# Two queue positions exchanged in an attention tower: the product with the values and the scores on TensorE, the heads' evictions and the relu on ScalarE

## Chip, core and metric

The kernel runs on one core of one Trainium2 chip. The metric is the device time of one execution in microseconds (us).

## What is computed

64 images of 196 tokens (patches of 16x16x3 pixels) go through patch embedding and layer norm, one quantised attention layer with a residual, and a layer of routed experts with a residual. What matters here is the attention, cut from the reference:

```
q = fake_quant(q, s_q, -4, 3) * scale          # 12 heads of 16 columns
k = fake_quant(k, s_k, -4, 3)
v = fake_quant(v, s_v, -4, 3)
attn = einsum('bhnd,bhmd->bhnm', q, k)         # the scores
attn = fake_quant(attn / N, s_attn, 0, 7)      # clipped at 0 and 7, rounded; no softmax
out = einsum('bhnm,bhmd->bhnd', attn, v)       # the product with the values
out = fake_quant(out, s_after, -4, 3)
return out @ Wproj.T + bproj
```

## The kernel before

The images are taken in 16 groups of four (784 tokens). A group passes through three stages in three consecutive passes, so that in each pass one group is embedded and normalised (`one`), the next older one goes through attention (`two`), and the oldest through projection and experts (`three`). There are 18 passes. A pass has 24 slots, and written-out tables say in which slot each piece of work is issued. Every engine runs through the slots in its own program order, and semaphores tie the engines together. An engine never passes over an instruction that waits.

A unit of attention is two heads of one image; a group has 24 units, so slot s of a pass holds unit s. The work of a unit:

- TensorE, `qk`, in even slots: 8 small matmuls make the scores of two units, s and s+1. They fill all four banks of `scores_ps`, so `qk` waits until ScalarE has read the two units before (`act_relu`).
- ScalarE, `relu`, in every slot: the scores of unit s times a scale, clipped at 0, rounded into `relu16`. It waits for `qk` and for VectorE's reading of the unit before last.
- VectorE, `quantise`, one slot later: clips at 7 and writes `prob`, a ring of 8 units.

When the six units of an image are in `prob`, their product with the values follows. The table `AV = [8, 14, 20, 26]` gives its slots for the four images; 26 is slot 2 of the next pass. All four slots are even, so each of them holds a `qk` as well, as long as a group is in stage two:

- TensorE, `av`: 24 small matmuls write the heads of one image into `near_ps`. It waits for `prob`, for the values, and for `near_ps` to be empty. That bank is shared with the patch embedding (`embed`), whose tiles ScalarE moves out as the last thing of a slot (`embed_evac`, L861).
- ScalarE, `heads_evac`: two activations, `o16_a` (L920) and `o16_b` (L921), move the heads out.
- VectorE, `clip_heads`, at the end of the slot, clips them for the projection.

In the slot before three of the four `av` (slots 1, 7 and 13) an embedded tile ends on TensorE and is moved out by ScalarE. In slot 20 `near_ps` has long been empty.

The rest of TensorE's program order in a slot, behind `qk` and `av`: the first layer of the experts (`up`, L777), transposes (`turn`, L663), query, key and value rows (`step`, L641), embedding (L650, its last matmul L655), the routing (L751 to L753), `down` (L787), `project` (L741). Behind `relu` and `heads_evac`, ScalarE has `gelu` (L932), the copies of the transposed rows (L876, L886), `norm1` (L867), `step_evac` (L908, L913) and `embed_evac`. VectorE has among others the split of transposed rows (L1151), which waits for ScalarE's copies.

Of the kernel before, what the change touches and what calls it, by code (L numbers as in the profile page):

```python
# [117 lines left out]
def stages(i):  # L118

    return [Group(i - back) if 0 <= i - back < GROUPS else None for back in range(3)]  # L120


def wait(eng, sem, value):

    if value > 0:
        eng.wait_ge(sem, value)
# [106 lines left out]
def at(slots, slot):  # L233
    return [t for t, s in enumerate(slots) if s == slot]
# [7 lines left out]
def second_at(table, two, three, slot):  # L242

    return [(g, g.first2 + t) for g, s in ((two, slot), (three, slot + SLOTS)) if g for t in at(table[g.n2], s)]
# [7 lines left out]
def heads_at(two, three, slot):  # L252
    return [(g, n) for g, s in ((two, slot), (three, slot + SLOTS)) if g for n in at(AV, s)]
# [41 lines left out]
def vit_tower_kernel(nc, x, tok_w, tok_b, ln_w, ln_b, w_qkv, w_proj, s_q, s_k, s_v, s_attn,  # L295
# [5 lines left out]
    with ctx:  # L301
# [179 lines left out]
        for i in range(GROUPS + 2):  # L481
            one, two, three = stages(i)
# [13 lines left out]
        for i in range(GROUPS + 2):  # L496
            one, two, three = stages(i)
# [36 lines left out]
        def empty(eng, *user):  # L534

            if user in USER_BEFORE:
                eng.wait_ge(*USER_BEFORE[user])
# [40 lines left out]
        def is_first(g):  # L578
            return g.offset == 0
# [40 lines left out]
        def _(pe):  # L620
            ident = const_sb[0:TT, C_IDENT:C_IDENT + TT]

            def router_product():

                come(pe, 3)
                pe.wait_ge(rows_out, EVACS)
                pe.matmul(product_ps[:, 0:EXPERTS], encw[:, 0:128], sww[:, :], start=True, stop=True)
                pe.matmul(product_ps[:, EXPERTS:2 * EXPERTS], encw[:, 128:EMBED + LO], sww[:, :],
                          start=True, stop=True)
                pe.matmul(product_ps[0:TT, 2 * EXPERTS:3 * EXPERTS], encb[:, 0:1].broadcast_to([HIDDEN, TT]),  # L630
                          sww[:, :], start=True, stop=True).then_inc(set_pe, 1)
# [25 lines left out]
            def turn(kind, tile):  # L657
                src, made = (xn2, dve_xn2) if kind == 1 else (xn3, dve_xn3)

                pe.wait_ge(made, tile + 1)  # L660
                wait(pe, dve_lo, TURN_NO[kind, tile])
                rows = src[:, tile % 2]
                pe.transpose(turn_ps[:, 0:TT], rows[:, 0:128], ident)  # L663
                pe.transpose(turn_ps[0:LO, TT:2 * TT], rows[:, 128:EMBED], ident).then_inc(turned, 1)  # L664
# [47 lines left out]
            def unit_of(pair, odd):  # L712

                return 2 * odd + pair // 2 if pair < 4 else 4 + odd

            def av(g, n):

                pe.wait_ge(prob_out, g.count(SLOTS, PAIRS * (n + 1)))
                pe.wait_ge(v_clip, g.count(GI, n + 1))
                empty(pe, "heads", g.offset, n)  # L720
                def product(row, col, pair, odd, c, start, stop):
                    u = PAIRS * n + unit_of(pair, odd)
                    return pe.matmul(near_ps[row:row + 32, col:col + SEQ], v_pad[:, 2 * n + c, pair, odd],  # L723
                                     prob[:, u % RING, pair % 2, c * SEQ:(c + 1) * SEQ], start=start, stop=stop)

                for odd, c in itertools.product(range(2), repeat=2):
                    for pair in range(4):
                        product(32 * pair, 0, pair, odd, c, odd + c == 0, odd + c == 2)
                for c in range(2):
                    for pair, odd in itertools.product(range(4, PAIRS), range(2)):  # L730
                        last = product(64 * (pair - 4) + 32 * odd, SEQ, pair, odd, c, c == 0, c == 1)
                last.then_inc(av_made, 1)
# [59 lines left out]
            def body(one, two, three):  # L792
                for s in range(SLOTS):

                    if one and is_first(one) and s == min(FIRST_STEPS):
                        pe.wait_ge(set_dve, SET_ATTENTION)
                    if two and is_first(two) and s == ROUTER_PRODUCT:
                        router_product()
                    if two and is_first(two) and s == PROJ[two.n2][0]:
                        pe.wait_ge(set_dve, SET_ALL)  # L800
                    if two and s % VISIT == 0:
                        qk(two, s // VISIT)
                    for g, n in heads_at(two, three, s):
                        av(g, n)
                    if three and s <= LAST_EMBED:
                        for n in at(UP, s):
                            up(three, n)
                    for g, tile in second_at(TURN3, two, three, s):
                        turn(2, tile)
                    for tile in first_at(TURN2, one, s):  # L810
                        turn(1, tile)
                    if one and s in FIRST_STEPS:
                        step(one, FIRST_STEPS[s])
                    work = embeds_of(one, s) if one else []
                    ahead = 0 if any((k - s) % SLOTS == 0 for k in AV) else 1
                    for tile, j in work[:ahead]:
                        embed(tile, j)
                    if three and s > LAST_EMBED:
                        for n in at(UP, s):
                            up(three, n)  # L820
                    if three:
                        for part in at(ROUTE, s):
                            route(three, part)
                    if two and s in SECOND_STEPS:
                        step(two, SECOND_STEPS[s])
                    if s > LAST_EMBED:
                        for tile in third_at(DOWN, three, s):
                            down(three, tile)
                    if three:
                        for part in at(SPREAD, s):  # L830
                            spread_choice(three, part)
                    for g, tile in second_at(PROJ, two, three, s):
                        project(g, tile)
                    for tile, j in work[ahead:]:
                        embed(tile, j)
                    if s <= LAST_EMBED:
                        for tile in third_at(DOWN, three, s):
                            down(three, tile)
# [13 lines left out]
        def _(act):  # L852
# [63 lines left out]
            def heads_evac(g, n):  # L916
                cols = slice(SEQ * n, SEQ * (n + 1))
                act.wait_ge(av_made, g.count(GI, n + 1))
                wait(act, heads_clip, g.count(GI, n + 1 - GI))
                act.activation(o16_a[:, cols], near_ps[:, 0:SEQ], ACT.Identity, scale=c_out[:, :])  # L920
                act.activation(o16_b[:, cols], near_ps[:, SEQ:2 * SEQ], ACT.Identity,  # L921
                               scale=c_out[:, :], bias=one_row[:, :]).then_inc(heads_out, 1)
# [11 lines left out]

            def body(one, two, three):
                for s in range(SLOTS):
                    if two:
                        relu(two, s)
                    for g, n in heads_at(two, three, s):
                        heads_evac(g, n)  # L940
                    if three and s <= LAST_EMBED:
                        for n in at(UP, s):
                            gelu(three, n)
                    if two and is_first(two) and s == PROJ[two.n2][0]:
                        come(act, 3)
                    for g, tile in second_at(TURN3, two, three, s):
                        high_experts(g, tile)
                    for tile in first_at(TURN2, one, s):
                        high_rows(tile)
                    for tile in first_at(NORM1, one, s):  # L950
                        norm1(tile)
                    if one and is_first(one) and s == min(FIRST_STEPS):
                        act.wait_ge(set_dve, SET_ATTENTION)
                    if one and s in FIRST_STEPS:
                        step_evac(one, FIRST_STEPS[s])
                    if three and s > LAST_EMBED:
                        for n in at(UP, s):
                            gelu(three, n)
                    if two and s in SECOND_STEPS:
                        step_evac(two, SECOND_STEPS[s])  # L960
                    for tile in first_at(EVAC1, one, s):
                        embed_evac(tile)
# [425 lines left out]
```

## Time and profile before

| | |
|---|---|
| median of 3 runs | 998.43 us (997.61 to 999.94) |
| the profiled execution | 998.46 us, of which the span is 996.7 us |
| TensorE matmul busy | 907.5 us, 91% of the span |
| VectorE busy | 743.0 us, 75% |
| ScalarE busy | 702.9 us, 71% |
| GpSimd busy | 510.8 us, 51% |
| mean granted clock of TensorE | 0.972 of full speed |

Busy time is summed over instructions. Matmuls overlap in the pipeline, so the busy share of TensorE is not its share of peak. "Idle" is the time an engine stood still ahead of an instruction, with the instruction that released it; "issue" is idle time with no releaser in sight.

### The profile page before, as it was taken

Reading aid. Unit: us, or ns where it says so; the run is one execution under the profiler, and the core shown is the slowest. Engines: PE = TensorE matmul, PEld = TensorE weight load, DVE = VectorE, ACT = ScalarE, POOL = GpSimd, SP = SyncE. Lnnn points to the kernel's source line nnn. Section 1 sums busy time; section 2 is a strip of 40 time slices with the busy share of each in tenths; the row PEclk is TensorE's granted clock in tenths of the full one; section 3 lists DMA queues with packets and bytes.
Section 4 is the critical chain, followed back from the end, with each engine's and each line's share of the span. In section 5 each row is a group of like instructions: output and inputs, shape, how many; then the busy total and the mean of one; then the engine's idle time right before and its main releaser. Section 6 shows DMA issues by size and latency. Waiting matters only on the chain.

```text
span 996.7 us, 24830 instructions
## 1 busy us (share of the span) xinstructions
PE 907.5 (91%) x8170; PEld 785.2 (79%) x8170; DVE 743.0 (75%) x2855; ACT 702.9 (71%) x1516; POOL 510.8 (51%) x890
## 2 busy tenths in 40 slices
PE   5678999999999999998889899999999999999877
PEld 4566888888888888877677788888888888887766
DVE  4677878788788778777676777878878877878563
ACT  1367877777878777776566777777787877777652
POOL 4434564637465564636527456463746556463332
PEclk9797999999999999999999999999999999999889
DMA  7321121212121121212102112121202111000000
GB/s 228 105 64 34 49 64 41 61 45 74 32 69 49 53 65 41 61 45 68 44 25 73 32 53 65 41 64 42 77 29 69 50 53 49 10 13 13 14 13 28
DMA packets 31395, 52.52 MB, mean 53 GB/s; under 512 B 4653, under 2 KB 17949, under 8 KB 31269
## 3 DMA queue, kind: packets, MB, share of 16 engines
q1 hardware_dynamic: 31268, 50.94, 16.7%
q8 instruction: 67, 1.10, 0.5%
q14 instruction: 60, 0.48, 0.2%
HBM read 41.30 MB, written 9.63 MB: 51 GB/s over the span
## 4 chain that ended last, share of the span: by engine, by line
PE 34%; DVE 6%; ACT 6%; issue 5%; POOL 1%; DVEq 0%; ACTq 0%; POOLq 0%
PE mixed_ps L787 7%; PE near_ps L650 6%; PE mixed_ps L777 6%; PE mixed_ps L641 5%; PE scores_ps L708 2%; ACT relu L897 2%; PE near_ps L723 1%; PE turn_ps L663 1%; ACT hid L932 1%; ACT o_b L921 1%; DVE h L1222 1%; PE turn_ps L664 1%; PE mixed_ps L741 1%; DVE k_b L1182 1%; PE mixed_ps L742 1%
## 5 line engine op out<-in xcount | busy, mean ns | idle before, releaser
L897 ACT ACTIVATE relu<-scores_ps,c_prob 98x784 uint16<-98x784 f32 x384 | 348.8, 909 | 139.2 <-PE scores_ps L708 117.3
L650 PE MATMUL near_ps<-we,x_sb 128*128 128x192 f32 x1176 | 258.4, 341 | 12.5 <-DMA const_sb<-in_const 8.2
L978 POOL TENSOR_TENSOR ve<-mv,const_sb 128x1 f32<-128x1 f32 x294 | 60.3, 205 | 360.9 <-DVE mv L1319 357.1
L650 PEld LDWEIGHTS near_ps<-we,x_sb 128*128 128x128 f32 x1176 | 195.2, 196 | 19.1 <-DMA const_sb<-in_const 8.2
L991 POOL TENSOR_TENSOR expd<-econst,below 128x8 f32<-128x8 f32 x98 | 161.9, 1666 | 49.6 <-DVE below L1249 49.6
L981 POOL TENSOR_TENSOR rs<-ve,const_sb 128x1 f32<-128x1 f32 x294 | 173.9, 591 | 23.0
L1160 DVE TENSOR_SCALAR prob<-relu 98x784 bf16<-98x784 uint16 x384 | 151.1, 394 | 9.4 <-ACT relu L897 1.2
L787 PE MATMUL mixed_ps<-w_sb,hid 128*128 128x192 f32 x784 | 145.8, 330 | 0.0
L787 PEld LDWEIGHTS mixed_ps<-w_sb,hid 128*128 128x128 f32 x784 | 125.5, 191 | 1.4
L1135 DVE TENSOR_SCALAR xn<-h,mv,rs 128x192 f32<-128x192 f32 x196 | 74.1, 378 | 33.9 <-POOL rs L981 33.7
L932 ACT ACTIVATE hid<-mixed_ps,b_sb 128x384 f32<-128x384 f32 (+1 forms) x128 | 73.0, 586 | 36.2 <-PE mixed_ps L777 35.7
L1121 DVE BATCH_NORM_STATS2 st<-h 128x6 f32<-128x192 f32 x196 | 70.1, 357 | 10.8 <-POOL h L1000 6.9
L663 PE MATMUL turn_ps<-const_sb,xn 128*128 128x128 f32 x196 | 60.2, 307 | 17.6 <-DVE xn L1135 7.8
L996 POOL TENSOR_TENSOR m<-n,lnw 128x192 f32<-128x192 f32 x98 | 59.0, 602 | 33.1 <-ACT n L867 32.5
L908 ACT ACTIVATE rows<-mixed_ps,inv_rows 128x392 int16<-128x392 f32 x96 | 55.9, 582 | 24.6 <-PE mixed_ps L641 24.1
L867 ACT ACTIVATE n<-y,nb,rs 128x192 f32<-128x192 f32 x98 | 52.8, 539 | 23.1 <-DVE nb L1116 23.0
L1289 DVE SCALAR_TENSOR_TENSOR out_sb<-mixed_ps,pmax,h 128x192 f32<-128x192 f32 x98 | 40.9, 418 | 35.3 <-PE mixed_ps L787 32.5
L1000 POOL TENSOR_TENSOR h<-m,lnb 128x192 f32<-128x192 f32 x98 | 58.7, 599 | 7.7
L861 ACT ACTIVATE y<-near_ps 128x192 f32<-128x192 f32 x98 | 32.0, 326 | 42.0 <-PE near_ps L655 38.9
L708 PE MATMUL scores_ps<-q_a,k_a 32*98 32x196 bf16 x1024 | 49.0, 266 | 12.7 <-ACT relu L897 12.3
L741 PE MATMUL mixed_ps<-wp_a,o_a 128*128 128x192 f32 x196 | 55.7, 309 | 3.5 <-DVE o_b L1209 1.2
L663 PEld LDWEIGHTS turn_ps<-const_sb,xn 128*128 128x128 f32 x196 | 27.9, 143 | 39.0 <-DVE xn L1135 20.4
(155 smaller groups left out, 2208.2 us busy)
## 6 DMA issues: line engine op xcount, KB each, us to landing
x_sb<-in_x SPq DMA_DIRECT2D x98, 384.0 KB, 3.0
out<-out_sb SPq DMA_DIRECT2D x98, 96.0 KB, 1.6
we<-in_tok_w SPq DMA_DIRECT2D x1, 576.0 KB, 4.3
w_sb<-in_w SPq DMA_DIRECT2D x1, 384.0 KB
hid<-in_w_qkv SPq DMA_DIRECT2D x1, 288.0 KB, 5.5
hid<-in_w_qkv SPq DMA_DIRECT2D x2, 144.0 KB, 5.7
hid<-in_w SPq DMA_DIRECT2D x1, 256.0 KB
hid<-in_w SPq DMA_DIRECT2D x2, 128.0 KB
```

The costliest lines, as they stand in the source:

```text
L650: pe.matmul(dst, x_sb[:, tile % X_RING, j], we[:, j], start=j == 0, stop=False)
L663: pe.transpose(turn_ps[:, 0:TT], rows[:, 0:128], ident)
L708: last = pe.matmul(scores_ps[0:KEYS, bank, c * SEQ:(c + 1) * SEQ], keys, q[rows, n * SEQ:(n + 1) * SEQ], start=True, stop=True)
L741: pe.matmul(dst, o_a[:, cols], wp_a[:, j], start=j == 0, stop=False)
L787: last = pe.matmul(dst, hid[:, m, cols], w2_sb[:, m], start=False, stop=m == FC - 1)
L897: act.activation(relu16[:, u % 2], scores_ps[0:KEYS, 2 * (u % VISIT):2 * (u % VISIT) + 2, 0:2 * SEQ], ACT.Relu, scale=c_prob[0:KEYS, :]).t ...
L932: act.activation(hid[:, m, cols], bank[:, 0:cols.stop - cols.start], ACT.Gelu, bias=b1_sb[:, m:m + 1]).then_inc(gelu_out, 1)
L981: pool.tensor_tensor(rs[:, t], ve[:, t], const_sb[0:TT, C_HALFNEG:C_HALFNEG + 1], ALU.pow).then_inc(rs_sem, 1)
L991: pool.tensor_tensor(expd[:, t], econst[:, t], below[:, t], ALU.pow).then_inc(pool_exp, 1)
L1121: dve.bn_stats(st[:, tile % NT], src[:, tile % H_RING]).then_inc(st_sem, 1)
L1135: dve.tensor_scalar(dst[:, tile % 2], src[:, tile % H_RING], mv[:, t, 0:1], rs[:, t], ALU.subtract, ALU.mult).then_inc(dst_sem, 1)
L1160: dve.tensor_scalar(prob[:, u % RING], relu16[:, u % 2], 7.0, None, ALU.min).then_inc(prob_out, 1)
```

## The change

In a slot that has both, `av` is issued ahead of `qk` on TensorE, and `heads_evac` ahead of `relu` on ScalarE. No instruction is added or removed, and no table is changed.

```diff
@@ TensorE, body @@
+                    for g, n in heads_at(two, three, s):
+                        av(g, n)
                     if two and s % VISIT == 0:
                         qk(two, s // VISIT)
-                    for g, n in heads_at(two, three, s):
-                        av(g, n)
@@ ScalarE, body @@
                 for s in range(SLOTS):
+                    for g, n in heads_at(two, three, s):
+                        heads_evac(g, n)
                     if two:
                         relu(two, s)
-                    for g, n in heads_at(two, three, s):
-                        heads_evac(g, n)
```

## Rows read from the trace of the kernel before

**Rows 1.** The page's first part: busy us, share of the span, instructions.

```profile
PE 907.5 (91%) x8170; PEld 785.2 (79%) x8170; DVE 743.0 (75%) x2855; ACT 702.9 (71%) x1516; POOL 510.8 (51%) x890
```

**Rows 2.** Stages: stretch, length, busy time by engine, PEclk (granted clock), DMA.

```profile
121.00:177.00 56.00, 53.89 (x514) 47.29 (x510) 44.65 (x175) 43.45 (x95) 30.87 (x55) 1.00 0.18 54
461.00:532.00 71.00, 59.58 (x513) 50.63 (x505) 47.56 (x180) 45.17 (x99) 33.34 (x59) 0.95 0.14 43
```

**Rows 3.** Groups by line: busy us, mean ns | idle before, releasers.

```profile
L897 ACT ACTIVATE relu<-scores_ps,c_prob 98x784 uint16<-98x784 f32 x384 | 348.8, 909 | 139.2 <-PE scores_ps L708 117.3 <-DVE prob L1160 19.3
...
L723 PE MATMUL near_ps<-prob,v_pad 98*32 98x196 bf16 x1536 | 45.2, 252 | 8.0 <-ACT y L861 6.3 <-DVE v_pad L1193 0.2 <-DVE prob L1160 0.2
```

**Rows 4.** Timeline, slots 1 to 3: start us, duration us, engine, line, [idle before].

```profile
217.86 0.25 PE L655 MATMUL near_ps<-rows,first 128*128 128x192 bf16 x1
...
218.04 0.38 PE L708 MATMUL scores_ps<-q_a,k_a 32*98 32x196 bf16 x8
...
218.15 0.33 ACT L861 ACTIVATE y<-near_ps 128x192 f32<-128x192 f32 x1
...
218.62 0.70 PE L723 MATMUL near_ps<-prob,v_pad 98*32 98x196 bf16 x24 [0.21 <-ACT y L861]
...
219.25 0.28 PE L751 MATMUL mixed_ps<-wr_a,f_hi 128*128 128x16 f32 x1
...
219.37 0.42 ACT L920 ACTIVATE o_a<-near_ps,c_out 128x196 int16<-128x196 f32 x1
...
220.09 0.92 ACT L897 ACTIVATE relu<-scores_ps,c_prob 98x784 uint16<-98x784 f32 x1
...
220.77 0.35 DVE L1160 TENSOR_SCALAR prob<-relu 98x784 bf16<-98x784 uint16 x1
...
221.84 0.59 ACT L908 ACTIVATE rows<-mixed_ps,inv_rows 128x392 int16<-128x392 f32 x1 [0.84 <-PE mixed_ps L641]
```

**Rows 5.** Timeline, slots 20 to 22 of the same pass.

```profile
205.14 0.38 PE L708 MATMUL scores_ps<-q_a,k_a 32*98 32x196 bf16 x8
...
205.44 0.70 PE L723 MATMUL near_ps<-prob,v_pad 98*32 98x196 bf16 x24
...
205.57 0.91 ACT L897 ACTIVATE relu<-scores_ps,c_prob 98x784 uint16<-98x784 f32 x1 [1.19 <-PE scores_ps L708]
...
206.08 0.33 PE L663 MATMUL turn_ps<-const_sb,xn 128*128 128x128 f32 x1
...
206.38 0.42 ACT L920 ACTIVATE o_a<-near_ps,c_out 128x196 int16<-128x196 f32 x1
...
207.09 0.28 ACT L886 ACTIVATE f_hi<-turn_ps 128x128 fp32r<-128x128 f32 x1
...
208.80 0.37 PE L708 MATMUL scores_ps<-q_b,k_b 32*98 32x196 bf16 x8 [0.96 <-ACT relu L897]
```

**Rows 6.** Timeline, slots 8 to 10 of the pass before.

```profile
178.66 0.58 ACT L932 ACTIVATE hid<-mixed_ps,b_sb 128x384 f32<-128x384 f32 x1 [0.23 <-PE mixed_ps L777]
...
179.81 0.89 ACT L897 ACTIVATE relu<-scores_ps,c_prob 98x784 uint16<-98x784 f32 x1
...
180.95 0.38 PE L708 MATMUL scores_ps<-q_b,k_b 32*98 32x196 bf16 x8
```

**Rows 7.** Timeline, slots 14 and 15.

```profile
191.05 0.70 PE L723 MATMUL near_ps<-prob,v_pad 98*32 98x196 bf16 x24
...
192.87 0.58 ACT L932 ACTIVATE hid<-mixed_ps,b_sb 128x384 f32<-128x384 f32 x1 [0.25 <-PE mixed_ps L777]
...
193.56 0.39 PE L777 MATMUL mixed_ps<-f_hi,w_hi_a 128*128 128x384 f32 x1
```

**Rows 8.** Timeline, TensorE's waits in the first and the last pass with attention.

```profile
67.78 2.58 PE L650 MATMUL near_ps<-we,x_sb 128*128 128x192 f32 x7 [1.21 <-ACT o_b L921]
...
941.40 0.37 PE L708 MATMUL scores_ps<-q_a,k_a 32*98 32x196 bf16 x8 [0.83 <-ACT relu L897]
...
955.14 0.36 PE L741 MATMUL mixed_ps<-wp_a,o_a 128*128 128x192 f32 x1 [1.21 <-DVE o_b L1209]
```

## The prediction

> **What bounds the kernel.** I read the page's first part, then the stages, then the groups by line, and last the timeline round each place where both pieces of work meet. The first part says that TensorE is busy for 91% of the span, far ahead of the others [rows 1]. The stages say that this is steady: apart from the start, the end and some 130 us in the middle, a pass takes 56 us, with TensorE busy for 53.9 of them at the full granted clock of 1.00 [rows 2]. So TensorE's own order is the clock of the kernel. A delay put into it stays, unless TensorE waits soon after for something that was not delayed too. The groups by line say where the two edited places stand. ScalarE stood idle 139 us ahead of its relus, 117 us of them for the scores, so it mostly runs behind TensorE and not ahead of it. `av` waited 6.3 us in all, for ScalarE's move of the embedded tile [rows 3].
>
> **The change, place by place.** No instruction comes or goes and SyncE's queue is untouched; the two exchanges are all. They happen 63 times: 16 in slot 8, 16 in 14, 16 in 20, and 15 in slot 2 (the last group's fourth product has no scores beside it). The durations, from the rows: from the start of `qk` to the start of what follows it, 205.14 to 205.44 = 0.30 us; from the start of `av` to the next, 205.44 to 206.08 = 0.64; `heads_evac` holds ScalarE from 219.37 to 220.09 = 0.72; a relu from 205.57 to 206.38 = 0.81 [rows 4, 5].
>
> *Slot 2.* The embedding's last matmul starts at 217.86. `qk` starts at 218.04 and runs while ScalarE moves the embedded tile out (218.15 to 218.48). `av` can't start before that bank is free: it starts at 218.62 and TensorE goes on at 219.25 [rows 4]. So before, `qk` lies in the shadow of a wait that has to be sat out anyway. With `av` first nothing covers that wait. `av` still starts at 218.62, `qk` follows at 219.25, and the rest goes on at 219.55: +0.30 us on TensorE. ScalarE: the heads start at 219.37 as before, since `av` ends as before, but ScalarE stands idle until then and the relu is still to come. Relu 2 ends at 220.09 + 0.91 = 221.00 and relu 3 starts at 220.90. ScalarE's next work, the rows at 221.84, waited 0.84 us for TensorE, and this hides relu 3 up to 221.71. Without that cover the path would get 0.81, not 0.30. On VectorE, `quantise` at 220.77 would have to wait until 221.04, +0.27 [rows 4]. Both stay within TensorE's +0.30.
>
> *Slot 8.* The same picture, +0.30. ScalarE has less cover: gelu waited 0.23 us [rows 6], so it moves by 0.81 - 0.23 = 0.58 at most, and some 0.5 where TensorE's product comes 0.3 later anyway. Relu 9 then ends at about 180.70 + 0.5 = 181.2, and the next `qk` would start at 181.25 without it. I take +0.31.
>
> *Slot 14.* `av` starts at 191.05 either way and `qk` costs +0.30. But gelu moves from 192.87 to about 193.32, ends near 193.90, and TensorE's third `up` in the row, at 193.56, writes the bank which that gelu empties. It starts near 193.96 in place of 193.86: +0.40 in all [rows 7].
>
> *Slot 20.* `near_ps` is empty here, so the exchange is free on TensorE itself. ScalarE is the path: it is idle until `qk` ends, does relu 20 at 205.57, the heads at 206.38, goes on at 207.09, and the `qk` of slot 22 has waited 0.96 us for relu 21 at the end of that row [rows 5]. Now ScalarE waits for `av`. `av` is done 0.70 after its start, at 205.84, the heads start at 205.89, which is 0.32 behind the 205.57 of before; heads and relu take as long in either order, so relu 21 and the `qk` of slot 22 come 0.32 later. TensorE waits 1.28 instead of 0.96: +0.32.
>
> The sum for a pass is 0.30 + 0.31 + 0.40 + 0.32 = 1.33 us. Of the 63 places 56 lie in the 14 passes between the start and the end: 14 x 1.33 = 18.6 us. The bounds for one place: nothing, if the delay is taken up by slack behind it, and 0.72 to 0.81, if the relu's whole delay reaches TensorE. I stay near 0.3 because all the waits between these places that I followed are themselves started by TensorE, so they move with it.
>
> **The tile shapes.** One transition isn't in this trace: `av` (98 rows by 32 columns of the array) straight into `qk` (32 by 98) and from there into full matmuls. Eight score matmuls as such take about 0.13 us: the group lasts 0.38, and one matmul of 196 columns 0.25, which is the mean of L723 [rows 3, 5]. The other 0.17 of the 0.30 passes before the next starts. If that 0.17 overlapped behind `av`, three places would cost 0.13 each, and a pass 0.8. I take 0.30, since `qk` straight into `av`, the same switch the other way round, shows the full 0.30 at 205.14 [rows 5]. The Trainium skill, page "TensorEngine Tiling (Array Packing)", section "Key Properties", says that changing the tiling mode drains the engine. By that rule every one of the three switches keeps its 0.17 and the pass costs 1.33 us; without it the cost is 0.8, or 11 us for the 14 passes. The trace agrees as far as it goes, by the 0.17 behind both kinds.
>
> **Start and end.** Here the heads come sooner and something waits for them. The embedding at 67.78 waited 1.21 us for the heads' move. At 955.14 the projection waited 1.21 us for heads that start 0.75 and not 1.24 us after the slot's begin: 0.5 us gained at each. At 941.40 `qk` waited 0.83 us for a relu, time that `av` now fills, worth some 0.4 us [rows 8]. The other four places I put at +0.5 together. That makes -0.9 us for start and end.
>
> The sum is 18.6 - 0.9 = 17.7 us. On the profiled execution, 998.46 us (1.8 of them outside the span and untouched), that makes 1016.2; the median of the runs is 998.43, the same within 0.03. I predict **1016 us**.
>
> **Rivals.**
>
> *Faster: `av` fills the waits for the relu.* `qk` waits for ScalarE to empty `scores_ps`, and `av` could run meanwhile and hand over the heads sooner. It decides if, at these four places, the relu is what TensorE waits for. At slot 20, `qk` doesn't wait, and at slots 2, 8 and 14 `av` waits for ScalarE longer than `qk` does. If slack behind took up all the delay and only the gains of start and end were left, it would be 998.4 - 1.4 = 997; with 0.3 us gained in slots 14 and 20 of each of the 14 passes as well (8.4), 989. Against it speaks that TensorE is busy 53.9 of 56 us [rows 2].
>
> *No change.* TensorE's delay is taken up, since the 0.96 us wait in slot 22 is there in every pass. That would need relu 21 not to move; but the row shows that the chain behind it begins with TensorE's scores. 998.
>
> *Half.* The switch from `av` to `qk` overlaps, or one of the four places is absorbed: 0.8 us a pass, 14 x 0.8 - 0.9 = 10.3, so 1009.
>
> *More.* The relu's delay reaches TensorE in slots 8 and 14, through `qk` in slot 10 or through VectorE, which splits transposed rows only after ScalarE's copies: 0.5 us for each place, 56 x 0.5 = 28, less 0.9: 1026.
>
> *The clock.* In the slow stretch in the middle the granted clock is 0.95, after long waits of TensorE, while it is 1.00 in passes whose longest wait is 0.96 [rows 2, 5]. If 1.28 us were enough to make it fall in each pass, the stretch at half clock would cost more than 1 us a pass, so over 1030.
>
> **How the numbers follow.** The forecast, between 1.1 and 1.6 us a pass (1013 to 1020), has 0.50; half 0.17; more 0.14; the clock 0.04; no change 0.06; faster 0.07; the rest, 0.02, is slower by only a few us. The range leaves out the cases without a delay and those of the clock: it reaches from 0.5 us a pass less the ends' gain (1004) to that of the whole 0.5 us a place (1026). I can tell 0.2%, or 2 us, from no change. Faster 0.07, same 0.06, slower 0.87.
>
> **What would show it.** In the profile after: L723 idle ahead of it grows from 8 us by some 0.3 us in each of three places of a pass, to 20 us or more, nearly all released by L861; the `qk` of the same slot follows 0.63 us behind `av` without a wait; the matmul behind comes 0.30 us after `qk`; TensorE's wait for relu in slot 22 is 1.28 us; heads start 0.75 us after the slot's first small matmul in slot 20; the steady pass takes 57.3 us and not 56.0. The prediction is wrong if steady passes still take 56.0 us, if `qk` behind `av` takes under 0.2 us, or if TensorE gets new waits for L932, L897 or VectorE's splits of 0.3 us or more.

## The result, and the profile after

The changed kernel takes 1020.99 us in the median of 4 runs (1019.71 to 1023.24), beside 998.02 us for the kernel before in the runs taken with it. The ratio is 1.0235, with a 95% interval of 1.0208 to 1.0262: slower. The forecast was 1016 us in a range of 1004 to 1026. One run in this document, the slowest with TensorE's exchange alone, was in a slower state and is left out of its ratio.

The page of the changed kernel, first part:

```profile
span 1021.5 us, 24830 instructions
...
PE 911.7 (89%) x8170; PEld 787.5 (77%) x8170; DVE 743.4 (73%) x2855; ACT 697.7 (68%) x1516; POOL 511.9 (50%) x890
```

The work is the same; each engine is busy about as long as before [rows 1], and the span is 24.8 us longer. So most of the difference is idle time. By stages, a steady pass and the slow stretch in the middle (stretch, length, busy time by engine, granted clock, DMA):

```profile
181.00:238.50 57.50, 54.05 (x508) 47.23 (x507) 44.65 (x175) 43.05 (x95) 31.00 (x55) 1.00 0.18 53
```

```profile
459.00:536.00 77.00, 64.14 (x548) 54.74 (x547) 52.83 (x200) 46.16 (x105) 35.96 (x64) 0.94 0.15 45
```

The steady pass grew from 56.0 to 57.5 us with the same TensorE work (53.9 and 54.1 us), still at the full clock [rows 2].

The groups by line show where TensorE and ScalarE now stand idle:

```profile
L920 ACT ACTIVATE o_a<-near_ps,c_out 128x196 int16<-128x196 f32 x64 | 27.1, 424 | 64.1 <-PE near_ps L723 64.1
...
L723 PE MATMUL near_ps<-prob,v_pad 98*32 98x196 bf16 x1536 | 44.7, 250 | 23.2 <-ACT y L861 22.3
```

TensorE's idle time ahead of `av` rose from 8.0 to 23.2 us, 22.3 of them for the embedded tile [rows 3]; ScalarE's ahead of the heads rose from 0.6 to 64.1 us.

Slot 2 after, TensorE, ScalarE and VectorE (start us, duration, [idle before]):

```profile
224.29 0.25 PE L655 MATMUL near_ps<-rows,first 128*128 128x192 bf16 x1
...
224.57 0.33 ACT L861 ACTIVATE y<-near_ps 128x192 f32<-128x192 f32 x1
...
225.04 0.70 PE L723 MATMUL near_ps<-prob,v_pad 98*32 98x196 bf16 x24 [0.51 <-ACT y L861]
...
225.67 0.38 PE L708 MATMUL scores_ps<-q_a,k_a 32*98 32x196 bf16 x8
...
225.79 0.42 ACT L920 ACTIVATE o_a<-near_ps,c_out 128x196 int16<-128x196 f32 x1 [0.89 <-PE near_ps L723]
...
225.98 0.28 PE L751 MATMUL mixed_ps<-wr_a,f_hi 128*128 128x16 f32 x1
...
227.53 0.36 DVE L1160 TENSOR_SCALAR prob<-relu 98x784 bf16<-98x784 uint16 x1 [0.25 <-ACT relu L897]
...
228.09 0.18 DVE L1243 TENSOR_TENSOR logit<-mixed_ps,logit 128x24 f32<-128x24 f32 x1
...
228.42 0.33 PE L741 MATMUL mixed_ps<-wp_a,o_a 128*128 128x192 f32 x1
```

From the embedding's last matmul to `av` it is 0.75 us, as before (0.76 in [rows 4]). The scores that used to run inside this wait now come 0.63 us behind `av`, and the routing starts 0.31 us behind them: 1.69 us from L655 to L751, 1.39 before. That is +0.30 us on TensorE at this place. At the same time VectorE waited 0.25 us for the relu, a wait that it did not have. Which of the two delays reaches the rest of the pass, these rows alone don't say.

Slots 20 and 22 after:

```profile
211.25 0.70 PE L723 MATMUL near_ps<-prob,v_pad 98*32 98x196 bf16 x24
...
211.89 0.38 PE L708 MATMUL scores_ps<-q_a,k_a 32*98 32x196 bf16 x8
...
212.01 0.42 ACT L920 ACTIVATE o_a<-near_ps,c_out 128x196 int16<-128x196 f32 x1 [1.49 <-PE near_ps L723]
...
212.73 0.91 ACT L897 ACTIVATE relu<-scores_ps,c_prob 98x784 uint16<-98x784 f32 x1
...
215.24 0.38 PE L708 MATMUL scores_ps<-q_b,k_b 32*98 32x196 bf16 x8 [1.28 <-ACT relu L897]
```

The heads start 0.76 us after the slot's first matmul, and TensorE's wait in slot 22 is 1.28 us, where [rows 5] has 0.96.

Slot 14 after (PEld is the weight load of the third product):

```profile
196.71 0.70 PE L723 MATMUL near_ps<-prob,v_pad 98*32 98x196 bf16 x24 [0.51 <-ACT y L861]
...
198.98 0.59 ACT L932 ACTIVATE hid<-mixed_ps,b_sb 128x384 f32<-128x384 f32 x1
...
199.62 0.19 PEld L777 LDWEIGHTS mixed_ps<-f_hi,w_hi_a 128*128 128x128 f32 x1 [0.28 <-ACT hid L932]
```

Gelu ends at 198.98 + 0.59 = 199.57, and the third product, which overwrites its bank, starts at 199.62 (its matmul and its weight load alike). That is 2.91 us behind `av`, and 2.51 before [rows 7].

To place the loss I took the starts of all `qk` from both traces and compared each interval from one to the next, averaged over five steady passes (passes 4 to 8 of the 18). The growth per place, in us, with that of each experiment below; the intervals around a place are summed, and a row's places can miss its sum by some 0.01. The two rows of one exchange alone are not at full clock throughout; what that does to them is said below.

| kernel | slot 2 | slot 8 | slot 14 | slot 20 and 22 | a pass |
|---|---|---|---|---|---|
| after | +0.33 | +0.34 | +0.46 | +0.32 | +1.46 |
| ScalarE's exchange alone | +0.33 | +0.35 | +0.45 | +0.90 | +2.03 |
| TensorE's exchange alone | +2.29 | +0.99 | +0.77 | +0.63 | +4.68 |
| both, slot 2 only | +0.33 | 0 | 0 | 0 | +0.34 |
| both, slot 14 only | 0 | 0 | +0.45 | 0 | +0.45 |
| both, slot 20 only | 0 | 0 | 0 | +0.32 | +0.32 |
| both, short relu, against its pair | +0.16 | +0.21 | +0.29 | -0.17 | +0.49 |
| heads of slot 20 out in slot 21 | 0 | 0 | 0 | +0.69 | +0.68 |

### The profile page after: what moved, and what is told of

It reads as the page before. It is cut to its first block, busy times and chain, and to the rows that moved or that the text cites. A ratio compares the mean times of both kernels' runs of the same rounds, so it can differ in the third digit from the quotient of the medians.

```text
span 1021.5 us, 24830 instructions
## 1 busy us (share of the span) xinstructions
PE 911.7 (89%) x8170; PEld 787.5 (77%) x8170; DVE 743.4 (73%) x2855; ACT 697.7 (68%) x1516; POOL 511.9 (50%) x890
## 4 chain that ended last, share of the span: by engine, by line
PE 34%; ACT 7%; DVE 6%; issue 5%; POOL 1%; DVEq 0%; ACTq 0%; POOLq 0%
PE mixed_ps L787 7%; PE near_ps L650 6%; PE mixed_ps L777 6%; PE mixed_ps L641 5%; ACT relu L897 3%; PE near_ps L723 2%; PE scores_ps L708 2%; PE turn_ps L663 1%; ACT hid L932 1%; DVE k_b L1182 1%; PE turn_ps L664 1%; DVE prob L1160 1%; DVE h L1222 1%; ACT y L861 1%; PE mixed_ps L741 1%
## 5 line engine op out<-in xcount | busy, mean ns | idle before, releaser
L650 PE MATMUL near_ps<-we,x_sb 128*128 128x192 f32 x1176 | 261.9, 345 | 12.1 <-DMA const_sb<-in_const 8.4
L978 POOL TENSOR_TENSOR ve<-mv,const_sb 128x1 f32<-128x1 f32 x294 | 63.8, 217 | 379.6 <-DVE mv L1319 376.0
L650 PEld LDWEIGHTS near_ps<-we,x_sb 128*128 128x128 f32 x1176 | 198.0, 198 | 18.9 <-DMA const_sb<-in_const 8.4
L981 POOL TENSOR_TENSOR rs<-ve,const_sb 128x1 f32<-128x1 f32 x294 | 171.6, 584 | 23.0
L1160 DVE TENSOR_SCALAR prob<-relu 98x784 bf16<-98x784 uint16 x384 | 151.2, 394 | 19.5 <-ACT relu L897 11.3
L996 POOL TENSOR_TENSOR m<-n,lnw 128x192 f32<-128x192 f32 x98 | 59.1, 603 | 33.3 <-ACT n L867 32.7
L920 ACT ACTIVATE o_a<-near_ps,c_out 128x196 int16<-128x196 f32 x64 | 27.1, 424 | 64.1 <-PE near_ps L723 64.1
L723 PE MATMUL near_ps<-prob,v_pad 98*32 98x196 bf16 x1536 | 44.7, 250 | 23.2 <-ACT y L861 22.3
L723 PEld LDWEIGHTS near_ps<-prob,v_pad 98*32 98x32 bf16 x1536 | 31.0, 96 | 39.7 <-issue 28.2
```

Source lines behind the costliest of these rows:

```text
L650: pe.matmul(dst, x_sb[:, tile % X_RING, j], we[:, j], start=j == 0, stop=False)
L978: pool.tensor_tensor(ve[:, t], mv[:, t, 1:2], const_sb[0:TT, C_EPS:C_EPS + 1], ALU.add).then_inc(ve_sem, 1)
L981: pool.tensor_tensor(rs[:, t], ve[:, t], const_sb[0:TT, C_HALFNEG:C_HALFNEG + 1], ALU.pow).then_inc(rs_sem, 1)
L1160: dve.tensor_scalar(prob[:, u % RING], relu16[:, u % 2], 7.0, None, ALU.min).then_inc(prob_out, 1)
```

## The experiments

**The halves of the change.** TensorE's exchange alone:

```diff
 # TensorE
+ for g, n in heads_at(two, three, s): av(g, n)
  if two and s % VISIT == 0: qk(two, s // VISIT)
- for g, n in heads_at(two, three, s): av(g, n)
 # ScalarE: unchanged, relu ahead of heads_evac
```

> Only TensorE's order is exchanged; ScalarE still does the relu ahead of the heads. My theory (TensorE pays in slots 2, 8 and 14 because nothing covers the wait for the embedded tile any more, and in slot 20 because ScalarE starts later): slot 2 +0.3 us, slot 8 +0.5, slot 14 +0.7, slot 20 +0.63 (the relu now starts behind the scores, which are 0.63 later), 2.1 us a pass, +30 us in all, some 1028. The rival (the exchange on ScalarE costs, since it pushes the relu back; the exchange on TensorE is free): a change of less than 5 us.

Measured: 1073.71 us (1061.78 to 1078.8, 4 runs), ratio 1.0727 (1.0665 to 1.079). Far from free, so the rival falls, but it is also more than twice what I expected. Slot 2 alone shows 2.29 us in the table:

```profile
226.73 0.70 PE L723 MATMUL near_ps<-prob,v_pad 98*32 98x196 bf16 x24 [0.51 <-ACT y L861]
...
227.78 0.91 ACT L897 ACTIVATE relu<-scores_ps,c_prob 98x784 uint16<-98x784 f32 x1 [1.20 <-PE scores_ps L708]
...
228.60 0.42 ACT L920 ACTIVATE o_a<-near_ps,c_out 128x196 int16<-128x196 f32 x1
...
229.45 0.26 DVE L1208 TENSOR_SCALAR o_a<-o_a 128x196 fp32r<-128x196 int16 x1 [1.42 <-ACT o_b L921]
...
229.56 0.56 PE L650 MATMUL near_ps<-we,x_sb 128*128 128x192 f32 x2 [0.73 <-ACT o_b L921]
```

`av` is done at 227.43, but ScalarE first waits for the late scores and does their relu, and starts on the heads only at 228.60. VectorE waits 1.42 us for the heads, and the next embedding 0.73 us for `near_ps`. That last wait was 1.4 us in all before, and is 19.5 us here, in the list of waits:

```profile
PE near_ps L650 <- ACT o_b L921: 19.5, 29, 1.8
```

And the clock has a share: this pass is not at 1.00.

```profile
181.00:241.60 60.60, 55.36 (x504) 48.43 (x503) 43.76 (x173) 42.74 (x93) 30.36 (x54) 0.97 0.17 51
```

Four of the five passes averaged in the table have a stretch at the lower clock, which begins behind slot 2. In the fifth, at 1.00 throughout, slot 2 costs 1.12 us (0.30 for the scores and 0.73 for the wait make most of it) and the pass 3.58. So about half of slot 2's 2.29 us is the clock, and the order of the two engines is the rest. In this kernel TensorE's exchange alone loses more than twice what both together lose.

ScalarE's exchange alone:

```diff
 # ScalarE
+ for g, n in heads_at(two, three, s): heads_evac(g, n)
  if two: relu(two, s)
- for g, n in heads_at(two, three, s): heads_evac(g, n)
 # TensorE: unchanged, qk ahead of av
```

> Only ScalarE's order is exchanged; TensorE still does the scores first, which start in the shadow of the wait. My theory: slot 2 costs nothing (the wait for TensorE of 0.84 us ahead of the rows covers the relu), slot 8 +0.3 (relu 9 is late for the scores of slot 10), slot 14 +0.4 (gelu empties a bank late), slot 20 +0.63 (the heads wait for a product that starts 0.30 behind the scores): 1.3 us a pass, some 1017. The idle time ahead of the product with the values stays at 8 us. The rival (ScalarE's push of 0.7 to 0.8 us is what costs at all four places): slot 2 costs as much as the others, 0.3 or more.

Measured: 1029.17 us (1026.59 to 1030.93, 4 runs), ratio 1.0318 (1.03 to 1.0337). Here my theory fell in slot 2. TensorE keeps its covered scores (idle ahead of `av` 8.5 us in all), and still slot 2 costs 0.33 us, as much as in the changed kernel. Slots 8 and 14 also cost just what they cost there. The groups by line, first of the kernel before and then of this run, say through what:

```profile
L741 PE MATMUL mixed_ps<-wp_a,o_a 128*128 128x192 f32 x196 | 55.7, 309 | 3.5 <-DVE o_b L1209 1.2 <-ACT v L913 0.8 <-ACT rows L908 0.8
...
L777 PE MATMUL mixed_ps<-f_hi,w_hi_a 128*128 128x384 f32 x120 | 48.4, 403 | 2.2 <-DVE h L1222 2.0
```

```profile
L741 PE MATMUL mixed_ps<-wp_a,o_a 128*128 128x192 f32 x196 | 56.4, 312 | 5.7 <-DVE logit L1243 3.1 <-DVE o_b L1209 1.0 <-ACT rows L908 0.8
...
L777 PE MATMUL mixed_ps<-f_hi,w_hi_a 128*128 128x384 f32 x120 | 48.9, 408 | 6.3 <-ACT hid L932 3.1 <-DVE h L1222 2.0 <-DVE f_c L1270 1.0
```

New are the waits of the projection for `logit` and of the third product for gelu (`hid`). In slot 3 the projection writes the bank of the routing's product, which VectorE empties with its first two steps of the choice. In VectorE's order these stand behind `quantise` of unit 2, and that waits for the relu that the heads pushed back. The timeline of that pass, before (the pass of [rows 4]) and with ScalarE's exchange alone:

```profile
221.32 0.18 DVE L1243 TENSOR_TENSOR logit<-mixed_ps,logit 128x24 f32<-128x24 f32 x1
...
221.65 0.33 PE L741 MATMUL mixed_ps<-wp_a,o_a 128*128 128x192 f32 x1
```

```profile
225.08 0.36 DVE L1160 TENSOR_SCALAR prob<-relu 98x784 bf16<-98x784 uint16 x1 [0.25 <-ACT relu L897]
...
225.63 0.18 DVE L1243 TENSOR_TENSOR logit<-mixed_ps,logit 128x24 f32<-128x24 f32 x1
...
225.96 0.32 PE L741 MATMUL mixed_ps<-wp_a,o_a 128*128 128x192 f32 x1 [0.20 <-DVE logit L1243]
```

In all three orders the projection starts 0.33 us behind VectorE's second step: before (221.32 to 221.65), here (225.63 to 225.96) and in the changed kernel (228.09 to 228.42). So VectorE sets the start of the projection, and that is where slot 2's loss comes from.

In slot 8 it is the relu itself. Here too TensorE's scores of slot 10 wait for relu 9:

```profile
182.83 0.90 ACT L897 ACTIVATE relu<-scores_ps,c_prob 98x784 uint16<-98x784 f32 x1
...
183.87 0.37 PE L708 MATMUL scores_ps<-q_b,k_b 32*98 32x196 bf16 x8 [0.28 <-ACT relu L897]
```

They start 1.04 us behind the relu's start, as in the changed kernel (185.58 and 186.62); before it was 1.14, and they didn't wait [rows 6].

**Does TensorE pay by itself?** After this run the uncovered scores could have been innocent. To take ScalarE's part away I shortened the relu in both orders: it reads 16 of the 392 columns of each bank, which leaves out most of the scores, and takes about 0.2 to 0.3 us.

```diff
-act.activation(relu16[:, u % 2], scores_ps[0:KEYS, 2 * (u % VISIT):2 * (u % VISIT) + 2, 0:2 * SEQ], ACT.Relu,
+act.activation(relu16[:, u % 2, :, 0:16], scores_ps[0:KEYS, 2 * (u % VISIT):2 * (u % VISIT) + 2, 0:16], ACT.Relu,
+# and relu16 is set to zero once at the start
```

The order of before:

> The kernel before, but the relu reads 16 of the 392 columns of each score bank, so it takes some 0.2 us and not 0.9. It leaves out most of the attention's first step and is there only as the pair of the next run. With ScalarE this light the waits of TensorE for the relu and the wait in slot 22 should be gone: a pass of 53 to 55.5 us. TensorE's wait for the embedded tile ahead of the product with the values should still be there, about 0.2 us.

The order of after:

> The kernel after, with the same short relu. What heads first cost the relu shrinks from 0.7 to 0.8 us to about 0.1, so ScalarE's and VectorE's share of the loss is gone, and what is left is TensorE's own. First theory (TensorE pays by itself, since the scores no longer run in the shadow of the wait): +0.30 us against its pair in each of slots 2, 8 and 14, 0.9 us a pass, 13 us in all. Second theory (only ScalarE's exchange costs, as the run with ScalarE's exchange alone lets one think): under 0.1 us in each place, under 4 us in all.

One run each: 982.78 and 984.59 us. Two single runs don't tell this difference from none. The traces do: steady passes of 55.30 and 55.79 us, +0.49. (The start of the second trace happened to be 1.4 us shorter.) Neither theory's number is met. Slot 2, order of before:

```profile
217.63 0.25 PE L655 MATMUL near_ps<-rows,first 128*128 128x192 bf16 x1
...
219.02 0.28 PE L751 MATMUL mixed_ps<-wr_a,f_hi 128*128 128x16 f32 x1
...
221.09 0.18 DVE L1245 TENSOR_TENSOR logit<-mixed_ps,logit 128x24 f32<-128x24 f32 x1
...
221.39 0.19 PEld L741 LDWEIGHTS mixed_ps<-wp_a,o_a 128*128 128x128 f32 x1 [0.15 <-issue]
```

Order of after:

```profile
216.40 0.25 PE L655 MATMUL near_ps<-rows,first 128*128 128x192 bf16 x1
...
218.09 0.28 PE L751 MATMUL mixed_ps<-wr_a,f_hi 128*128 128x16 f32 x1
...
219.85 0.18 DVE L1245 TENSOR_TENSOR logit<-mixed_ps,logit 128x24 f32<-128x24 f32 x1
...
220.24 0.19 PEld L741 LDWEIGHTS mixed_ps<-wp_a,o_a 128*128 128x128 f32 x1
```

My reason for the pair was wrong in one point: heads first still push the relu back, relu 2 by 1.6 us (its start is 0.61 and 2.22 us behind L655). But it now ends before VectorE comes to it, and VectorE's second step stands where it stood, 3.46 and 3.45 us behind L655. So ScalarE's part is out of slot 2 all the same. At the place itself TensorE does pay 0.30 us (L655 to L751: 1.39 and 1.69). But the projection in slot 3 had stood idle for 0.15 us ahead of its weights, and in the second order it did not; so 0.15 of the 0.30 comes back there. In slot 14 nothing comes back (+0.29). In the steady passes of neither order does TensorE wait for relu or gelu at these three places, so what is left there is its own. In slot 20 this pair gains 0.17. So TensorE's share exists, and in slot 2 it is smaller than the rows at the place say.

**One place at a time.** The exchange of both engines under a condition, here slot 2:

```diff
+ if s == 2: av(...)                      # TensorE; ScalarE: heads_evac(...)
  if two and s % VISIT == 0: qk(...)      # ScalarE: relu(...)
+ if s != 2: av(...)
```

> Both exchanges in slot 2 only. My theory: +0.31 us a pass, all of it on TensorE between the end of the embedding and the routing's first matmul; the other places as before; 15 places, +4.6 us, 1003. The rival (the places act on one another and only together make 1.46 us a pass): under 0.15 us a pass.

Measured: 1003.61 us (4 runs), ratio 1.0066 (1.0048 to 1.0083), +0.34 us a pass. The size is as expected. Both engines are exchanged here, so the run doesn't say through which the loss comes; I had expected all of it on TensorE.

> Both exchanges in slot 14 only. My theory: +0.47 us a pass, of which 0.30 are the scores behind the product and 0.17 a new wait of TensorE for the gelu that empties the bank of its third product with the first layer's weights; +7 us in all, 1005. The rival (only the uncovered scores cost): +0.30 us a pass, no wait for gelu.

Measured: 1002.18 us (4 runs), ratio 1.0049 (1.0033 to 1.0066), +0.45 us a pass, with the expected wait for gelu (0.28 us). The pass is as expected; the time, 4.6 us above the kernel before and not 7, is under it.

> Both exchanges in slot 20 only, where near_ps is long empty. My theory: TensorE loses nothing at the place itself, ScalarE starts 0.32 us later, and the wait of TensorE for relu 21 in slot 22 grows from 0.96 to 1.28 us: +0.32 us a pass, 16 places, +5 us, less some 0.5 us gained where the last pass waits for the heads: 1002. The rival (the products fill TensorE's wait and the heads are out sooner, so slot 20 by itself gains): 0.2 us or more gained a pass, 993 or less.

Measured: 1003.28 us (6 runs), ratio 1.0063 (1.0046 to 1.008), +0.32 us a pass. The rival falls: where `near_ps` is free and `av` fills TensorE's time, the exchange still loses.

The three and slot 8's 0.34 add up to 1.45, the changed kernel's 1.46. The places don't act on one another.

**A better version?** If ScalarE's chain in slots 20 and 21 holds up slot 22, the heads could be taken out of it.

```diff
-HEADS_EVAC = AV
+HEADS_EVAC = [8, 14, 21, 26]      # read by ScalarE and by VectorE's clip_heads
 # ScalarE, slot 21: heads_evac behind step_evac; TensorE's order as before
```

> The order of before, but the heads of slot 20 are moved out by ScalarE at the end of slot 21 and clipped by VectorE in slot 21. My theory (in slot 20 ScalarE's chain scores, relu 20, heads, relu 21 holds up the scores of slot 22): the wait of 0.96 us in slot 22 falls to 0.25, -0.7 us a pass, -11 us, 987. The rival (another wait takes its place, for the rows that ScalarE moves out behind relu 21, or for the heads in the projection of slot 22): less than -0.2 us a pass.

Measured: 1011.96 us (5 runs), ratio 1.0158 (1.0129 to 1.0187): slower. The scores of slot 22 did come 0.53 us sooner, and then the rival happened (line numbers are 4 to 6 higher in this kernel):

```profile
209.85 0.37 PE L712 MATMUL scores_ps<-q_b,k_b 32*98 32x196 bf16 x8 [0.43 <-ACT relu L901]
...
210.92 0.26 DVE L1214 TENSOR_SCALAR o_a<-o_a 128x196 fp32r<-128x196 int16 x1 [0.89 <-ACT o_b L925]
...
211.27 0.35 DVE L1228 TENSOR_TENSOR h<-mixed_ps,h 128x192 f32<-128x192 f32 x1
...
211.77 0.33 PE L745 MATMUL mixed_ps<-wp_a,o_a 128*128 128x192 f32 x1 [0.39 <-DVE h L1228]
```

VectorE waits 0.89 us for the late heads, the residual is queued behind, and the projection waits for the residual. Taken together: +0.68 us a pass.

The same with `av` and the heads of slot 14 put behind the first product of the experts' layer and its gelu:

> As the run before it, and in slot 14 the product with the values is issued behind the first product of the experts' layer on TensorE, and the heads behind its gelu on ScalarE, which gives the wait for the embedded tile a cover of 0.9 us. My theory: another -0.15 us in slot 14 (the wait), and gelu 0.7 us sooner, so -0.15 to -0.3 us a pass beside the -0.7 of slot 20: 983 to 985. The rival (VectorE clips the heads later and its order passes the delay on): no gain beside slot 20, or a loss of up to 0.5 us a pass.

Measured: 1013.56 us (5 runs), ratio 1.0186 (1.0157 to 1.0214), +0.67 us a pass, slot 14 within 0.03 of before. No gain there. No version that I ran and that does all the work beats the kernel before.

## Why the prediction was right

The sign and the size were right: +1.33 us a steady pass forecast, +1.46 measured (1.37 to 1.53 in the twelve passes outside the middle). The mechanism was right in slot 20 and for gelu in slot 14. In slots 2, 8 and 14 the forecast put 0.30 us each on TensorE's uncovered scores, and there ScalarE's exchange alone costs as much as both. That the two are of like size is luck, and the sum came out right by it. By its steps:

*Slot 20*: +0.32 forecast, +0.32 measured, with the wait of 1.28 us in slot 22 that was named. Shown by the run of slot 20 alone.

*Slot 14*: +0.40 forecast, +0.46 measured. The new wait for gelu is there. The run of slot 14 alone gives the same; 0.40 of it lies at the third product, the rest further on, which I did not follow. ScalarE's exchange alone gives +0.45 here, with TensorE's scores still covered, so the wait for gelu doesn't need the 0.30 us of the scores under it.

*Slot 8*: +0.31 forecast, +0.34 measured, and +0.35 with ScalarE's exchange alone. The relu's end is the gate for slot 10. The forecast had the relu 0.01 us behind TensorE's own delay of 0.30; TensorE's own, by the pair with the short relu, is 0.21.

*Slot 2*: +0.30 forecast, +0.33 measured, but for another reason. I put all of it on the uncovered scores and said that VectorE's +0.27 would stay inside. ScalarE's exchange alone costs the same 0.33, through `quantise`, the choice, and the bank that the projection waits for. I had followed the relu as far as VectorE and not to who waits for VectorE. The projection stands 3.79 us behind L655 before and 4.13 after, each time 0.33 behind VectorE's step; with the short relu, where TensorE's delay is alone, it stands at 4.02. The two delays run side by side, one on TensorE's order and one round by ScalarE, and the larger sets the place; they are not a sum. With the relu shortened, TensorE's own part is 0.16, 0.21 and 0.29 in slots 2, 8 and 14, under ScalarE's 0.33, 0.35 and 0.45 everywhere.

*The tile shapes*: `qk` follows `av` after 0.63 us and the full matmuls follow `qk` after 0.31, so each switch keeps its tail. The Trainium skill, "TensorEngine Tiling (Array Packing)", "Key Properties", says that changing the mode drains the engine; this trace agrees, and the cheaper case of 0.8 us a pass is out.

*Start and end*: -0.9 us forecast. The three waits that were named did shrink about as forecast: 1.21 to 0.72 us for the embedding (now at 70.48), 0.83 to 0.20 for the scores (964.76), 1.21 to 0.73 for the projection (977.39). The net isn't shown. The trace grew by 0.5 us in the first pass with attention and fell back by 1.3 behind the start of the last, -0.8 together, but the two executions differ in their clock there: before it was at 0.50 from 917.7 to 927.9, and the last pass after was at 1.00 up to 980. That the -0.8 is near the forecast is luck.

What the sum did not have, beside 0.13 us a pass, is the clock. The 24.8 us between the spans are, by the delay of the `qk` at the head of each pass: 2.9 before anything of the change is run, 0.5 in the first pass, 20.4 in 14 passes of 1.46, 2.2 more in the middle, and -1.3 at the end. Of the 2.9 us at the start, 2.0 arise in the second embedded tile, before:

```profile
13.46 2.19 PE L650 MATMUL near_ps<-we,x_sb 128*128 128x192 f32 x12 [0.51 <-ACT y L861]
```

and after:

```profile
13.60 4.18 PE L650 MATMUL near_ps<-we,x_sb 128*128 128x192 f32 x12 [0.51 <-ACT y L861]
```

The 4.18 us are what the first tile takes in both traces (4.21), so the second tile seems to have run at the lower clock (1.2 GHz) too; the granted clock of this trace isn't recorded so early. Most of the other 0.9 comes with a stretch at 0.50 near 42 us, which the trace before doesn't have. The orders are the same there, so this belongs to the execution and not to the change; 12 runs of the kernel before went from 992.3 to 1001.7 us. The middle, with more time at the lower clock (0.94 over its 77 us, 0.95 over 71 in [rows 2]), is where waits of TensorE were already over 2.5 us long. Its two passes took 136.8 us before and 141.9 after, but 139.0, 135.6 and 134.8 with the exchange in slot 2, 14 and 20 alone. So they vary by more than those 2.2 us from execution to execution, and what of them is the change's is not shown.

The rival of the clock, at 1.28 us of wait in each pass, did not come about: all steady passes stayed at 1.00. The rival with the relu's whole delay was not reached, though a delay on ScalarE is what binds at all four places. The faster rival was tried where it had its best chance, slot 20, and failed.

## What to carry to other kernels

Before putting work in front of something that runs in the shadow of a wait, ask what will stand in the shadow then. When two engines' orders are exchanged together, cost each alone as well: here each half by itself is worse than both, and at three of the four places ScalarE's half costs by itself what both cost, so that undoing TensorE's would have given nothing there. Follow a delayed instruction through every in-order engine to the one that sets the pace, to the last bank that somebody waits for, not only to the next idle time.

## What the runs showed of the hardware

A wait of TensorE's that comes once in each pass can cost clock as well, and it need not be much longer than one that doesn't. With 0.96 us in slot 22, and with 1.28, steady passes keep a granted clock of 1.00. With either exchange alone that wait is 1.59 us, here with ScalarE's:

```profile
212.79 0.38 PE L708 MATMUL scores_ps<-q_b,k_b 32*98 32x196 bf16 x8 [1.59 <-ACT relu L897]
```

With ScalarE's exchange the clock falls to 1.2 GHz right behind the scores that end this wait in 3 of the 12 steady passes, and such a pass takes 59.1 us in place of 57.8. That is why the table has +0.90 for slots 20 and 22, where a pass at full clock has +0.63. With TensorE's exchange 8 of the 12 have such a stretch, but at another place: behind the 0.73 us wait of the embedding at 229.56 shown above, which follows waits of 1.59 us (216.90) and 0.51 (226.73). In the other passes of both kernels the same waits cost no clock. In the last pass with attention of the changed kernel even a wait of 1.67 us, at 956.85, left it at 1.00. So the length of one wait doesn't decide it, and what does is not shown here. I had not expected 1.59 us to be enough at times.
